# Value products ahead of the last key block's transposes at each change of head pair

## The reference

```python
x = x + gnn(layernorm(x))          # two graph convolutions, relu between them
x = x + ffn(layernorm(x))
# in ffn, with h = layer norm of its input, 12 heads of 64:
q, k, v = h @ Wq, h @ Wk, h @ Wv
scores = where(causal, q @ k.T * 768 ** -0.5, -inf)
out = softmax(scores) @ v          # for each head
x = x + out @ Wp + bp
h2 = layernorm(x)
# each token goes to its best one of 8 experts (768 -> 3072 -> 768, relu)
x = x + expert_of_token(h2)
```

## Time and profile before

| | us |
|---|---|
| median of 3 runs | 891.88 |
| lowest, highest | 890.35, 893.12 |
| profiled execution | 887.97 |
| its span, first to last instruction | 886.4 |
| busy in the span: TensorE (PE), weight load (PEld) | 846.7, 817.1 |
| VectorE (DVE), ScalarE (ACT), GpSimd (POOL) | 715.6, 552.7, 78.2 |

### The profile page before, as it was taken

How to read it: one execution, slowest core, us unless ns; L and a number is a source line. 1 busy time by engine, 2 the same in 40 slices (tenths; PEclk the granted TensorE clock), 3 DMA queues, 4 the chain that set the end, 5 groups by cost and what they waited for, 6 DMA issues and landing times.

```text
span 886.4 us, 14643 instructions
## 1 busy us (share of the span) xinstructions
PE 846.7 (96%) x5336; PEld 817.1 (92%) x5336; DVE 715.6 (81%) x1095; ACT 552.7 (62%) x785; POOL 78.2 (9%) x85
## 2 busy tenths in 40 slices
PE   6999999989899998999999999999999999999997
PEld 6899999989788887899889999999999999999996
DVE  6999676873577788754888897998989899898985
ACT  4612342353577777613678787888878788787870
POOL 2000000230400000031600000000000000000050
PEclk9999999999999999999999999999999999999997
DMA  7030008153920032530699999999999999999973
GB/s 219 21 108 1 19 9 171 53 156 79 323 101 1 2 107 71 178 89 1 215 370 353 360 349 375 347 364 374 351 376 359 364 371 359 377 352 369 367 259 123
DMA packets 116232, 196.00 MB, mean 221 GB/s; under 512 B 34052, under 2 KB 83420, under 8 KB 116182
## 3 DMA queue, kind: packets, MB, share of 16 engines
q1 hardware_dynamic: 107988, 169.08, 56.4%
q0 software_dynamic: 6368, 24.19, 8.0%
q10 hardware_dynamic: 1826, 2.06, 0.8%
HBM read 177.40 MB, written 17.90 MB: 220 GB/s over the span
## 4 chain that ended last, share of the span: by engine, by line
PE 50%; DVE 24%; DMA 14%; ACT 6%; issue 6%; SPq 0%; DVEq 0%; ACTq 0%
DVE wlo L994 13%; DMA raw<-in_L_ffn_W 12%; PE ps L1486 11%; PE ps L1900 7%; PE ps L1881 7%; PE ps L1663 7%; PE ps L1739 3%; ACT whi L664 2%; PE ps L1567 2%; PE ps L1593 2%; PE ps L1702 2%; PE ps L1717 2%; PE ps L1515 2%; DVE hTT L992 1%; PE ps L1866 1%
## 5 line engine op out<-in xcount | busy, mean ns | idle before, releaser
L994 DVE TENSOR_TENSOR wlo<-raw,whi 128x2304 fp32r<-128x2304 f32 (+1 forms) x150 | 352.7, 2359 | 22.9 <-ACT whi L664 22.6
L664 ACT ACTIVATE whi<-raw 128x2304 fp32r<-128x2304 f32 (+1 forms) x152 | 300.7, 1980 | 79.5 <-DMA raw<-in_L_ffn_W 31.9
L1900 PE MATMUL ps<-whi,hTT 128*128 128x384 f32 x768 | 201.5, 339 | 0.9 <-ACT oh7T L664 0.9
L1900 PEld LDWEIGHTS ps<-whi,hTT 128*128 128x128 f32 x768 | 139.2, 188 | 1.2 <-ACT oh7T L664 1.2
L1881 PE MATMUL ps<-whi,hgh 128*128 128x384 f32 x384 | 133.1, 347 | 1.3 <-DVE hgl L994 1.3
L1881 PE MATMUL ps<-whi,hgl 128*128 128x384 f32 x384 | 129.1, 336 | 0.0
L1900 PE MATMUL ps<-wlo,hTT 128*128 128x384 f32 x384 | 129.0, 336 | 0.0
L1881 PE MATMUL ps<-wlo,hgh 128*128 128x384 f32 x384 | 128.4, 334 | 0.0
L1881 PEld LDWEIGHTS ps<-whi,hgh 128*128 128x128 f32 x384 | 72.2, 188 | 1.5 <-DVE hgl L994 1.5
L1900 PEld LDWEIGHTS ps<-wlo,hTT 128*128 128x128 f32 x384 | 72.3, 188 | 0.0
L1881 PEld LDWEIGHTS ps<-wlo,hgh 128*128 128x128 f32 x384 | 72.3, 188 | 0.0
(11 more groups left out here) (291 smaller groups left out, 1626.2 us busy)
## 6 DMA issues: line engine op xcount, KB each, us to landing
raw<-in_L_ffn_W SPq DMA_DIRECT2D x128, 1152.0 KB, 6.9
hs_d<-bc POOLq DMA_DIRECT2D x13, 384.0 KB, 6.4
raw<-in_L_gnn_W SPq DMA_DIRECT2D x4, 1152.0 KB, 5.8
hs<-hs_d POOLq DMA_DIRECT2D x8, 384.0 KB, 5.5
ys_d<-ysb POOLq DMA_DIRECT2D x7, 384.0 KB, 6.0
raw<-in_L_ffn_Wv SPq DMA_DIRECT2D x6, 384.0 KB, 5.4
raw<-in_L_ffn_Wq SPq DMA_DIRECT2D x12, 192.0 KB, 3.6
raw<-in_L_ffn_Wk SPq DMA_DIRECT2D x12, 192.0 KB, 3.6
```

Source lines behind the costliest of these rows:

```text
L664: act.activation(out_, in_, func).then_inc(s, 1)
L994: dve.tensor_tensor(out_, in_, hi_, ALU.subtract).then_inc(s, 1)
L1900: ins = mm(ps[0:CAP, 4 + half, 0:HB], l, rr, start=k == 0 and j == 0 and jj == 0, stop=k == FCH - 1 and j == JW - 1 and jj == 2)
```

## The change

At passes i = 5, 10, ... 30 TensorE does `next_pair(i)` and `values(i - 2)` ahead of `first_block(3)` (only at i = 30) and `turn_last(i - 1)`, and ScalarE does `normed(2 * i)` and `normed(2 * i + 1)` ahead of the copy of the fifth block. VectorE's order and all waits are the same.

```diff
@@ ScalarE
                 if 1 <= i <= STEPS:
                     turned(2 * i - 2)
                     turned(2 * i - 1)
-                    if i % C == 0:
-                        a.wait_ge(s_tr5, i // C)
-                        hi(pT_last(pT[0], i // C - 1), last_turned(i // C - 1), s_trh5)
                 if i < STEPS and i % C < SHORT:
                     normed(2 * i)
                     normed(2 * i + 1)
+                if 1 <= i <= STEPS and i % C == 0:
+                    a.wait_ge(s_tr5, i // C)
+                    hi(pT_last(pT[0], i // C - 1), last_turned(i // C - 1), s_trh5)
                 if i in UNIT_AT:
                     unit_hi(UNIT_AT[i])
@@ TensorE
                 if 1 <= i <= STEPS:
                     turn(2 * i - 2)
                     turn(2 * i - 1)
+                next_pair(i)
+                if i >= 2:
+                    values(i - 2)
                 if i == STEPS:
                     first_block(3)
                 if 1 <= i <= STEPS and i % C == 0:
                     turn_last(i - 1)
-                next_pair(i)
-                if i >= 2:
-                    values(i - 2)
```

## The result

| | us |
|---|---|
| the change, median of 7 runs (lowest, highest) | 883.19 (882.01, 885.82) |
| before, median of 7 runs (lowest, highest) | 890.35 (886.84, 893.12) |
| ratio, 95% interval | 0.9925 (0.9904 to 0.9947) |
| profiled execution of the change, its span | 885.82, 884.2 |

The 4 runs of before that were added brought its median from 891.88 to 890.35, so 1.5 us of the 4.6 us between 887.8 and 883.2 is the base's own scatter; the interval still doesn't hold the forecast ratio of 0.9954.

The account below looks back on a forecast made before the run. TensorE was taken to set the pace in the attention stage. Four changes of pair winning 4.0 us, plus 0.3, less 0.2, gave 4.1 us: median 891.88 to 887.8 us, range 885.3 to 890.9.

Parts of the forecast that it names:

- The bound and the wait: Attention stage: TensorE sets the pace; turn_last (L1724) waits 6.7 us in five places for VectorE's pTl subtraction.
- Values ahead cover it: Value products ahead of turn_last cover its old wait completely; scores come 1.33 us earlier at i = 5.
- site 1: The change of pair at i = 5, first of six numbered through i = 30; about 1.0 us won there.
- The next wait, of `turn(2i+1)` for pTl: Second transposes of the following step newly wait for VectorE's pTl, giving back 0.34 of 1.33 us.
- `normed` costs nothing where it now stands: On ScalarE, normed fits the gap before the fifth block's copy; left behind it, turn(2i) waits until about 254.75 us.
- Site 5 wins 0.3 us: Change of pair at i = 25: VectorE's later ql holds the value products, so only 0.3 us is won.
- Site 6 loses 0.2: Change of pair at i = 30: turn_last comes 1.5 us later behind the value products, losing 0.2 us.
- Sum 4.1 us: Whole gain over the six changes of pair: 4.0 + 0.3 - 0.2 = 4.1 us.
- All else follows TensorE: After the changes of pair, other engines and expert weights follow TensorE; the won time reaches the kernel's end.
- rival 2: Won time is given back further on, by late ScalarE and VectorE or the expert stage: 889.5 to 891.9 us; chance 0.18.
- Rival 4: Low clock at 418 to 421 us may hit products that count: 1.5 us lost, sum 2.6 us; chance 0.07.
- rival 1: The new wait of turn(2i+1) does not bind: 6 us or more won, 885.9 us; chance 0.10.

Follow-up runs that it names:

- e3: The change with ScalarE's order as before, only TensorE's part kept: median 883.24 us, ratio to before 0.9940; attention stage 137.1 us.
- e2: The change plus 18 unread products on TensorE behind the attention stage, about 4.2 us: median 887.81 us, ratio to before 0.9984.
- e1: The change again, unaltered, against the kernel before: median 882.7 against 888.52 us, ratio 0.9929; attention stage 136.6 us.
- e11: The change again, unaltered, one profile: attention stage 138.0 us.
- e4: The kernel before with only ScalarE's part of the change, TensorE's order as before: median 888.04 us, ratio 0.9997; attention stage 143.2 us.
- e7: The kernel before, unaltered, one more profile: attention stage 142.2 us.
- e5: The kernel before plus ten unread products in TensorE's idle time at i = 25: median 886.34 against 888.82 us, ratio 0.9974.
- e9: The change, with value products at i = 25 made to wait for VectorE's pTl: median 885.84 against 890.88 us, ratio 0.9955; stage 139.7 us.
- e10: A second profile of the kernel of e9: attention stage 139.7 us.
- e6: The change with turn_last back in place at i = 30 and ql ahead of the last weights in pass 24: median 881.24 us, ratio to before 0.9912.
- e12: e6 plus four unread products on TensorE ahead of turn(48) and turn(49): median 883.63 us, ratio to before 0.9928.

## Why the prediction was wrong

- *The bound and the wait* (L1724, five places): right; the wait is gone. It was about half of the waits in the stage (6.7 of 13.7 us), not over half.
- *Values ahead cover it, `turn_last` 0.23 us later at site 1*: right, 0.08 us plus the lead of 0.17.
- *The next wait, of `turn(2i+1)` for pTl, gives back 0.34 us*: right in place and kind. At site 1 0.54 - 0.12 = 0.42 us, which makes site 1 worth 0.83 us instead of 1.0.
- *`normed` costs nothing where it now stands*: right. That it would hold the next transposes back until about 254.75 if left (0.2 to 0.3 us a site, by the expectation of e3): wrong at sites 1 to 4, where nothing is lost (e3). The handover of 0.52 us was that of products out of a standstill and is 0.42 in a stream.
- *Site 5 wins 0.3 us*: mis-sized, 0.6, in part for the same reason and since ql starts 0.33 us behind pTl where the working had 0.42. *Site 6 loses 0.2*: 0.16.
- *Sum 4.1 us*: 4.25 in the pair of profiles. Its terms are off by up to 0.3 us, so a part of this closeness is luck.
- *All else follows TensorE*: the won time reaches the end (e2), so rival 2 falls, and no time was won in the expert stage (e1). Rival 4's loss didn't come where the earlier trace rows showed the low clock: from the last product of L1486 to the first of L1881 it takes 25.2 to 25.4 us with that fall (before, the change, e1, e11) and 25.2 without it (e4, e7).
- **The step that failed** is the one that made the sum of waits the whole price of standing idle, and so put the clock at nothing in the sum. Rival 4 looked for the clock only where the one profile showed it at 0.50, and only as a loss. In three of four profiles of TensorE's order of before the clock falls at site 5, which costs 1.4 us on the mean, against 0.35 with the change. Filling the idle time alone wins 2.3 us (e5), restoring it brings the fall back (e9, e10). With it the sum is 4.25 + 1.4 - 0.35 = 5.3 us, a ratio of 0.9940, inside both intervals (0.9904 to 0.9947 and 0.9902 to 0.9956). That the kernel before pays for its idle time at site 5 in clock is shown; how much of it the change wins back is worked out from four profiles a side, and the clock of e1's timed runs doesn't show it (0.9928 against 0.9925).
- What stays open: the middle of the two ratios is 1.1 us further on. Shares of falls from four profiles a side are rough, e5 alone allows for up to 3.8 us, and falls come at other places too (447 and 461 us, near the start of the expert stage, in one profile each of e6 and the change). By the profiles of site 5 the change spends 3.4 us less at the low clock on the mean, which should raise its mean clock by 0.0019, more than e1's interval holds. So the cause of what the result has beyond the 4.25 us stays open: the runs don't settle how much is clock and how much is chance.
- The range was too narrow below: it ended at rival 1's 885.9 less 0.6 us of scatter, and took nothing for a base of three runs that itself spread over 2.8 us. Those three were slow ones: of the 83 timed runs of before on record the median is 889.3, and 887.97, the profiled one, is in their fastest third. The 3.9 us between it and the 891.88 was in the main the base, and in part the fall that this profile lacked.

## What to carry to other kernels

A wait on TensorE can have two prices: its own length, and the chance that the clock falls with it, which then slows work that never waited (here 2.3 us at one place, by e5). Where waits crowd within a few microseconds, take several profiles of the same kernel and compare the clock column there, before the waits of a single one are added up. Even products that nobody reads can win time there (e5), though they won none in the kernel in which the longest wait was covered already (e12). And when a wait is covered, cost the handovers anew: here products in a stream handed over after 0.42 us, those out of a standstill after 0.52. Where the record has the mean clock of every timed run, compare it as well: it tells for a dozen runs what a profile tells for one.

## What the runs showed of the hardware

The granted clock went from 1.00 to 0.50 within or just behind waits of 0.8, 0.4 and 1.7 us at site 5, in 3 of 4 profiles of the same order on TensorE and not in the fourth, and once with waits of 0.8, 0.4 and 0.7 us (e11); it stayed there for 3.4 to 7 us. The Trainium skill, "TensorE: Matmul & The Clock Gate", section "What's actually happening", says that the chip judges activity at times of its own, which the kernel's start doesn't reset. The profiles fit that, though they can't show those times: the same instructions, the fall in some executions only. And the price was less than half of the time at half clock (1.2 to 2.3 us for 3.4 to 7 us). A likely reason, not tested, is that the stage there is not limited by TensorE's rate alone: it also waits for the other engines.
